# Decoder layer with gated delta rule: two attention grams and their products moved ahead of the MLP output, with four smaller moves in the queues

## The reference

```python
h = gated_delta_net(rms_norm(x), ...)       # 8 heads of 128, a recurrence over 512 tokens
x1 = x + h
m = rms_norm(x1)
y = square(relu(m @ W_fc)) @ W_proj         # the MLP of the first block
x = layernorm(x + x1 + y)
x = layernorm(x + windowed_attention(x, ctx))   # q = x; 8 positions, only 12 distinct keys
x = layernorm(x + mixture_of_experts(x))        # top 2 of 8 experts
# inside gated_delta_net, for each token t and head:
S = S * a_t;  delta = (v_t - k_t S) * b_t;  S = S + k_t^T delta;  o_t = q_t S / sqrt(128)
o = rms_norm(o) * o_norm_w * silu(gate);  h = o @ Wo
```

## Time and profile before

| | |
|---|---|
| time, median of 3 executions | 709.38 us (707.37 to 709.8) |
| profiled execution: its own time | 709.69 us |
| profiled execution: span from first to last instruction | 707.7 us |
| TensorE busy | 614.6 us (87%) |
| VectorE busy | 476.1 us (67%) |
| ScalarE busy | 407.2 us (58%) |
| GpSimd busy | 276.4 us (39%) |
| mean granted TensorE clock | 0.917 of full |

### The profile page before, as it was taken

One profiled execution on the slowest core, in us unless ns is written; L12 is line 12 of the kernel. 1 busy time (PEld: TensorE's weight loads), 2 busy tenths in 40 slices (PEclk: granted clock), 3 DMA queues, 4 the chain that ended last, 5 costly groups with the idle time before them and its releaser, 6 DMA issues.

```text
span 707.7 us, 14886 instructions
## 1 busy us (share of the span) xinstructions
PE 614.6 (87%) x5453; PEld 507.6 (72%) x5453; DVE 476.1 (67%) x1841; ACT 407.2 (58%) x723; POOL 276.4 (39%) x233
## 2 busy tenths in 40 slices
PE   2889999999998999999988999999899986339940
PEld 1456887888888778888787888887888875227740
DVE  4747944787888568888895787679657864513315
ACT  2734537898755587876646878756154653114413
POOL 3446002444444125426421443474212252226763
PEclk9999969999998999999999999999589997559985
DMA  8403130002105100020050002001401430032243
GB/s 253 154 1 75 46 70 1 2 1 46 31 1 115 17 1 15 2 49 24 21 128 3 1 16 46 16 20 48 81 1 44 161 87 10 13 72 27 24 93 107
DMA packets 78383, 34.02 MB, mean 48 GB/s; under 512 B 49968, under 2 KB 73849, under 8 KB 78184
## 3 DMA queue, kind: packets, MB, share of 16 engines
q1 hardware_dynamic: 74344, 30.89, 17.2%
q0 software_dynamic: 3968, 2.20, 2.3%
HBM read 20.04 MB, written 14.40 MB: 49 GB/s over the span
## 4 chain that ended last, share of the span: by engine, by line
PE 63%; DVE 18%; issue 6%; ACT 5%; DMA 4%; POOL 3%; SPq 1%; ACTq 0%; POOLq 0%; DVEq 0%
PE ps L681 21%; PE ps L646 6%; PE ps L722 4%; DVE prod L1868 4%; DVE blk_t L1875 4%; PE ps L834 3%; PE ps L1255 3%; PE ps L745 3%; PE ps L1245 3%; PE ps L822 3%; PE ps L1051 2%; PE ps L920 2%; PE ps L930 1%; POOL slots L595 1%; PE ps L941 1%
## 5 line engine op out<-in xcount | busy, mean ns | idle before, releaser
L490 POOL TENSOR_TENSOR att<-att,br 128x512 f32<-128x512 f32 x32 | 33.3, 1043 | 179.1 <-ACT att L1318 179.1
L471 POOL TENSOR_TENSOR of<-oss,mhalf 128x4 f32<-128x4 f32 x32 | 32.7, 1021 | 86.8 <-DVE oss L1762 86.2
L471 POOL TENSOR_TENSOR st<-st,mhalf 128x4 f32<-128x4 f32 (+1 forms) x23 | 22.4, 973 | 100.8 <-DVE st L1988 67.1
L1868 DVE TENSOR_TENSOR prod<-kn,blk_t 128x126 f32<-128x126 f32 (+35 forms) x244 | 53.0, 256 | 1.1 <-DMA kn<-n_blocks 1.1
L1875 DVE TENSOR_TENSOR blk_t<-blk_t,prod 128x126 f32<-128x126 f32 (+35 forms) x244 | 51.3, 249 | 0.1
L1264 ACT ACTIVATE uo<-ps 128x512 f32<-128x512 f32 x56 | 33.6, 600 | 20.0 <-PE ps L681 19.8
L1264 ACT ACTIVATE ogT<-ps 128x512 f32<-128x512 f32 x32 | 19.1, 596 | 42.9 <-PE ps L646 42.7
L681 PEld LDWEIGHTS ps<-kT 128*128 128x128 f32 x256 | 32.7, 192 | 14.9 <-issue 14.5
L681 PE MATMUL ps<-qT,kT 128*128 128x128 f32 x256 | 42.9, 324 | 0.4 <-DVE att L1767 0.4
L941 PEld LDWEIGHTS ps<-ones,kT 128*128 128x128 f32 x256 | 32.6, 192 | 11.5 <-issue 10.7
L1725 DVE SCALAR_TENSOR_TENSOR uo<-uo,of,gate_sb 128x128 f32<-128x128 f32 x128 | 38.6, 363 | 3.1 <-POOL of L471 3.1
(11 more groups left out here) (249 smaller groups left out, 1764.6 us busy)
## 6 DMA issues: line engine op xcount, KB each, us to landing
tt_blocks<-gate_sb SPq DMA_DIRECT2D x4, 512.0 KB, 3.0
TT<-tt_blocks SPq DMA_DIRECT2D x16, 128.0 KB, 2.6
Nm<-in_L_ffn_w SPq DMA_DIRECT2D x1, 2048.0 KB, 9.1
kn<-in_L_ffn_w SPq DMA_DIRECT2D x8, 256.0 KB, 4.5
n_blocks<-Nm SPq DMA_DIRECT2D x16, 96.0 KB, 2.6
kn<-n_blocks SPq DMA_DIRECT2D x4, 384.0 KB, 3.4
t_blocks<-blk_t SPq DMA_DIRECT2D x4, 384.0 KB, 2.3
slots<-qT SPq DMA_DIRECT2D x5, 274.0 KB, 3.9
```

The lines of the kernel that those rows point to most:

```text
L471: pool.tensor_tensor(out_ap, in_ap, mhalf[:, 0:n], ALU.pow).then_inc(done, 1)
L490: pool.tensor_tensor(heads(att[:, slot(kb, m)]), heads(att[:, slot(kb, m)]), bc(br[:, kb % 2, unit(m)].unsqueeze(2), [P, HG, P]), ALU.mult ...
L1868: counts.append(st.step(tt(pr, bc(bn_[:, j, i0:i0 + n].unsqueeze(2), [P, n, ncol]), bc(blk_t[:, j, 0:ncol].unsqueeze(1), [P, n, ncol]), AL ...
```

## The change

Nothing is added or removed; five groups of instructions change places in their engines' queues.

1. In `between`, TensorE makes grams 3 and 4 ahead of `post_y(b)` and no longer behind it, and VectorE does its products 3 and 4 right behind products 0 to 2, ahead of `post_a_stats(b)`.
2. In `levels`, `post_aT` (transposes on TensorE, copy on ScalarE) moves from between levels 1 and 2 to the place ahead of level 3.
3. At the end of `levels`, ScalarE's `l4_copy(b, 3)` comes ahead of `k_silu(kb, 1)`, which begins with the load of an activation table.
4. In `step`, VectorE's `gate_out(b, s-1)` comes ahead of the pieces of the older batch.
5. In `step` 3, `head_ss` (sums of squares of a later batch's x) comes behind `out_sum` and `state`.

```diff
@@ TensorE, between
                 q_sums(kb, 7)
+                for n in range(3, 5):
+                    qk_gram(kb, n)
                 if old:
                     post_y(b)
-                for n in range(3, 5):
-                    qk_gram(kb, n)
@@ TensorE, levels
                 qk_gram(b, 5)
-                if b >= 1:
-                    post_aT(b - 1)
                 pe.wait_ge(sm["tt_back"], b * 32 + 32)
                 level2(b, 0)
...
                 if key:
                     k_transpose(kb, 0)
+                if b >= 1:
+                    post_aT(b - 1)
                 pe.wait_ge(sm["t_zero"], b + 1)
@@ ScalarE, levels
-                if b >= 1:
-                    post_aT(b - 1)
                 for half in range(2):
...
                 if key:
                     kT_copy(kb, 0)
+                if b >= 1:
+                    post_aT(b - 1)
                 l3_copy(b, 0)
...
                 l4_copy(b, 1)
+                l4_copy(b, 3)
                 if key:
                     k_silu(kb, 1)
-                l4_copy(b, 3)
-                if key:
                     k_square(kb, 1)
@@ VectorE, step
                     rhs(b, s + 1)
+                if scan and s >= 1 and not last_key:
+                    gate_out(b, s - 1)
                 if kb >= B and s == 5:
                     post_x1(FIRST)
                     post_ssx(FIRST)
                 if old:
                     post_piece(b, s)
-                if nxt and s == 3:
-                    head_ss(kb + 1)
-                if scan and s >= 1 and not last_key:
-                    gate_out(b, s - 1)
...
                     out_sum(b, s)
                     if s < NU - GR:
                         state(b, s)
+                    if nxt and s == 3:
+                        head_ss(kb + 1)
                     out_norm(b, s)
@@ VectorE, between
                 eliminate(kb, aside)
-                for n in range(3):
+                for n in range(5):
                     att_mult(kb, n)
                 if old:
                     post_a_stats(b)
-                for n in range(3, 5):
-                    att_mult(kb, n)
                 if old:
                     post_a(b)
```

## The result

The changed kernel took 729.32 us (median of 6 runs, 727.0 to 729.99), the kernel before 708.95 us in the same job (6 runs, 705.0 to 713.41). The ratio is 1.0295, with a 95% interval of 1.0263 to 1.0328: slower by 20 us, where 14.5 were forecast.

What follows compares the result with a forecast made beforehand. Steps bound by TensorE's work, between them VectorE's chain from MLP sums to level 2. Chain 7.9, half clock 3.0 and 3.4, transposes 2.0, less 1.2 and 0.6: +14.5, 724 us; own range 719 to 730, reaching 716 to 733.

Steps and rivals of the forecast that it cites:

- The direction and the chain: Between steps: slower (0.95); late MLP sums, then VectorE's 7.5 us chain, put level 2 13.95 us after first product, +7.9 us.
- The clock: Rounds 1 to 3: half clock behind two new TensorE idle times, +3.0 us ahead of MLP sums, +3.4 on level 2.
- long half clock: Levels of rounds 1 and 2: TensorE stays at half clock throughout, some +7 a round, +28, 738 us; chance 0.15.
- Edit 3: End of levels: last inverse copy first gives back 0.4 us ahead of the scan in batches 0, 1 and 2, -1.2.
- Edit 4: Steps: nothing in batches 0 to 2; in the last batch about 0.3 us back in steps 2 and 5, -0.6.
- Edit 2: Levels: the transposes now stand ahead of level 3 on TensorE, +2.0 us over three rounds.
- Full clock: Rounds: stretches at half clock fall as before and cost nothing more, +8.1, 717.5 us; chance 0.2.
- The scaling runs free: VectorE's post_a: new times part it from GpSimd's products, 2.4 us back each round, -7.3, 716.6 us; chance 0.08.
- Faster: Between steps: level 1's wait goes, transposes leave the gap, level 2 starts when its work is ready, 701 us; chance 0.03.
- No change: Steps: the delay from between the steps is absorbed there; chance 0.02.

Runs made afterwards that it cites:

- c3: Changed kernel with VectorE making the scaling of post_a behind the copies of level 1 and product 5, no longer ahead: 711.91 us, ratio 1.0038 to the kernel before.
- b4: Kernel before with one added wait a round: GpSimd makes its products only after the scaling of post_a: 711.3 us, ratio 0.9982 to the kernel before.
- b3: Kernel before with only the inverse copy, gated output and head_ss moves (groups 3, 4 and 5): 710.62 us, ratio 0.9984 to the kernel before.
- a1: Kernel before with only grams 3 and 4 ahead of the MLP sums and all five products ahead of the sum over y_ps: 733.66 us, ratio 1.0247.
- c2: Kernel before with extra matmuls on TensorE whose results are not used: 704.58 us, ratio 0.9899 to the kernel before.
- a2: Changed kernel without the gram and product reordering (groups 2 to 5 alone): 718.39 us, ratio 1.0042 to the kernel before.
- b1: Changed kernel with extra unused matmuls in TensorE's idle times, 12 ahead of grams 3 and 4, 18 ahead of level 2: 717.61 us, ratio 1.01 to the kernel before.
- b2: Changed kernel with one added wait a round: GpSimd makes its products only after the scaling of post_a: 723.43 us, ratio 1.0177 to the kernel before.

## Why the prediction was right, and by how much it was off

**The direction and the chain: right.** The sum over `y_ps` starts the same 7.5 us ahead of the end of the first copy, as taken from the earlier trace rows; level 2 waits for that copy in all three rounds (4.52, 4.53 and 4.43 us, forecast 4.1); TensorE stands 2.65, 3.22 and 3.29 us ahead of the grams (forecast 2.6 to 3.1). At held clock the distance from first product to level 2 is 14.2 us against the 13.95 of the sum; over three rounds that is 8.6 us more than before, forecast 7.9. That this chain makes the loss is shown by c3: the scaling behind the copies, and 2.6 of the 3.0% are gone, the second gap and its half clock with them. One reading of the kernel before was wrong: the prediction says that VectorE's chain ended the wait for level 2 there. The copy was over 1.2 us earlier, and the wait ended with TensorE's own gram 5 and transposes at half clock, as b4 shows. The sum did not depend on it, since it set the new chain against the measured start of level 2.

**The clock: the term that was mis-sized.** The prediction took "a stretch of 3.4 us at half clock", 1.0 a round for the grams and MLP sums and 1.7 for level 2 in two rounds: 6.4 us. The stretches were 6.8 us long and more, in all three rounds. The two grams alone took 3.75 instead of 1.95. From the start of the grams to the start of level 1 it was 228.47 - 220.60 = 7.9 us in round 1 where 5.75 had been taken, so 2.1 and not 1.0; in rounds 2 and 3 it was 1.6 and 2.0, together 5.7 and not 3.0. Another 1.3 us are small gaps between the terms: the grams start 0.84 us and not 0.7 after the first product, and VectorE and TensorE each start 0.1 to 0.2 us after what they wait for. So the way from first product to level 2 grew by 15.0 us where 7.9 + 3.0 = 10.9 had been forecast: 4.1 of the 5.4 us that were missing, 2.7 of them by the clock. The other terms (level 2 at half clock, edits 2 to 5) came to +3.6 in the prediction, and the traces leave 19.9 - 15.0 = 4.9 for them. The trace of before had the longer kind of stretch too, 20.5 us in round 3; it was taken for an exception, and the rival *long half clock* had it as all or nothing. What came lies between the two.

**Edit 3: right in its own place, wrong behind it.** TensorE's timeline at the end of round 2 answers to the earlier trace rows; the wait is 1.16 us before and 0.77 now, as forecast. But the eight rows behind it take 1.61 us and not 1.13, and a window of the same trace shows why (granted clock 0.57):

```profile
399.12 1.61 PE L681 MATMUL ps<-vv,TT 128*128 128x128 f32 x8 [0.77 <-ACT TT L1471]
```

```profile
399.10:402.50 3.40, 3.38 (x18) 3.40 (x19) 0.85 (x3) 3.36 (x7) 0.00 (x0) 0.57 0.01 2
```

The prediction also took the steps as cover for ScalarE's `k_silu` and square, which now come 2 us later (L1300 is `k_silu`). They are not enough: 9 us later, in batch 1, TensorE waits 0.5 us for ScalarE's next `k_silu`, more than the 0.4 won (the row is below, with those of the steps). With edits 3 to 5 alone (b3) such a wait is there in all three batches, 0.7, 0.5 and 0.5 us; the kernel before, a1, b4 and c2, which have none of these edits, have it nowhere, and of the three only edit 3 moves ScalarE's work. So the forecast -1.2 was half spent again in the changed kernel, and more than spent in b3.

**Edit 4: right for the last batch's limit, slightly wrong in the steps.** The last batch's transposes no longer wait for the gated output (0.27 us, for a sum of the older batch, where it was 1.70), but the next state then ends the wait, as foreseen from the earlier trace rows, and for longer than foreseen, so that 0.1 us came back and not 0.3:

```profile
558.48 0.63 PE L646 MATMUL ps<-const,uo 128*128 128x128 f32 x4 [0.27 <-DVE a L2050]
...
562.07 1.13 PE L681 MATMUL ps<-vv,TT 128*128 128x128 f32 x8 [1.12 <-DVE St L1749]
```

In the steps of batch 1 the forecast was 0. TensorE's waits there (255 to 325 us: total, times, longest) answer to the earlier trace rows and show two small new ones: the 0.5 us for ScalarE's `k_silu`, and one for the router's logits that now stand behind the gated output on VectorE:

```profile
PE ps L681 <- ACT TT L1471: 0.8, 1, 0.8
PE ps L681 <- ACT kn L1300: 0.5, 1, 0.5
PE ps L646 <- DVE rt L2077: 0.3, 1, 0.3
```

**Edit 2: open.** Forecast +2.0. The pair a2 and b3 puts about 4 us on it with overlapping intervals; the pair of the changed kernel and edit 1 alone gives no price at all (1.0295 and 1.0247, with edits 3 to 5 between them). Where TensorE is at full clock differs from trace to trace, by 11 us at half clock between a2 and b3, and that is as large as what is looked for.

**The rivals.** *Full clock*, at 717.5 us, did not happen. b1 came near its condition, and its 717.61 us are near its number partly by luck: the rival left the stretches of the kernel before in place and b1 took nearly all of them away, and the kernel before of its job was 3 us slower than the 709.4 that the rival starts from. *The scaling runs free* did not happen: it took 3.31 us with GpSimd's products beside it. They start when GpSimd is through with the power, and b2 shows that they were the cause. The Trainium skill, "SBUF — State Buffer", "Who interferes with whom", has the two engines share a pair of ports; the 1.11 against 3.31 us agree with a contest of that kind, though no run looked at the port itself. *Faster* failed on the condition that it named: the sums would have had to end by 224.4, and they end near 228.5. *No change* failed since the steps absorb nothing: the first products of rounds 2 and 3 come 6.11 and 14.66 us later. *Long half clock* came in part, as said; the whole +28 did not.

What stays open is the price of edit 2, the split of the -1.1 us of edits 3 to 5, and why a stretch at half clock lasts 6.8 us in one place and 3.4 in another. That stretches follow idle time is not the whole of it either: the one at 218.00 in the earlier trace rows has no idle row ahead of it, TensorE was making sums of one column (L941).

## What to carry to other kernels

To move work earlier on one engine is to move what it passes later. Follow that work to its reader, and then look at what stands behind the reader's wait in its in-order queue: here it was a small copy that everybody waited for, and what took nearly all of the loss away (c3) was to put the long chain behind it, without undoing the order. Price an idle time on TensorE at its length and, as an upper bound, half of a long stretch at half clock behind it, less what of the stretch falls into the idle time; don't go by the shortest stretch seen in the profile. And ask of each instruction put behind another who reads it: a gain of 0.4 us on ScalarE was spent again by a wait of 0.5 us in the same batch. Where such a gap can't be closed, matmuls whose result nobody reads are worth a try: two small groups a batch made the kernel before 1.0% faster.

## What the runs showed of the hardware

- The kernel before itself took from 706.9 to 719.37 us in 47 executions of three jobs, a spread of 1.8%, and the granted clock moved with it, between 0.928 and 0.907. Over these executions a microsecond more at half clock (2 × (1 - clock) × time) went with about 0.37 us more of time. Not all of the clock's loss is on the path, but enough to hide a change of 1%.
- Half clock after idle times of 2.65 to 4.5 us lasted 6.8 us and 10.2 us; in the kernel before, two such stretches lasted 3.4 and 3.5 us after shorter idle times, and one 20.5. In the changed kernel the same wait of 0.77 us had one of about 3.4 us behind it in batch 2 and none in batch 1. Thirty bf16 matmuls of 512 columns in two gaps a batch brought the granted clock from 0.82 to 0.86 up to 0.97 to 1.00.
- Four scalings of 128x128 on VectorE took 3.31 us with GpSimd's products of 128x512 beside them, and 1.11 us when these waited.
